# One fused kernel, its opening rearranged: reciprocal copies, expert ticks and the second block's attention change places

## The reference

```
xn = layernorm(x)
s  = causal softmax attention(xn), 16 heads of 64, projected back to 128
f  = shared expert(xn) + routed expert(xn)   # top 1 of 8, gate = sigmoid(score), width 352
x  = x + s * silu(f)
xn = layernorm(x)
s  = linear attention(xn), 16 heads of 8, causal cumulative sums
f  = two layers of local attention (8 heads of 64, window 64) and gated MLP, on xn
x  = x + s * silu(f)
```

## Time and profile before

| what | us |
|---|---|
| three runs, median (lowest to highest) | 2015.17 (2014.45 to 2017.05) |
| the profiled execution | 2009.89 |
| its span, first to last instruction | 2008.1 |
| TensorE busy | 1741.9 |
| VectorE, ScalarE busy | 1256.6, 1191.0 |
| GpSimd busy | 851.9 |

### The profile page before, as it was taken

How to read it: one execution, slowest core, us unless ns; L and a number is a source line. 1 busy time by engine, 2 the same in 40 slices (tenths; PEclk the granted TensorE clock), 3 DMA queues, 4 the chain that set the end, 5 groups by cost and what they waited for, 6 DMA issues and landing times.

```text
span 2008.1 us, 38006 instructions
## 1 busy us (share of the span) xinstructions
PE 1741.9 (87%) x12538; PEld 1123.2 (56%) x12538; DVE 1256.6 (63%) x4105; ACT 1191.0 (59%) x3559; POOL 851.9 (42%) x985
## 2 busy tenths in 40 slices
PE   6699989998989888998999898988899798785776
PEld 5378754654566546664566456654566455463454
DVE  5244547566675567666766667666766665857764
ACT  3554547566756675657666575666665665453643
POOL 3622226533535343532554353533353255534640
PEclk9999999999989999999999999999999897897978
DMA  8256500000000000000000000000000000000000
GB/s 245 71 180 211 176 16 4 9 1 1 7 1 17 1 7 1 17 1 1 7 1 17 1 7 1 17 1 6 1 7 6 1 7 1 1 7 1 1 1 11
DMA packets 50012, 53.78 MB, mean 27 GB/s; under 512 B 6546, under 2 KB 42396, under 8 KB 49820
## 3 DMA queue, kind: packets, MB, share of 16 engines
q0 software_dynamic: 7808, 27.79, 4.3%
q1 hardware_dynamic: 42012, 23.56, 4.1%
HBM read 41.90 MB, written 9.44 MB: 26 GB/s over the span
## 4 chain that ended last, share of the span: by engine, by line
PE 46%; DVE 20%; ACT 8%; issue 7%; POOL 1%; DVEq 0%; ACTq 0%; POOLq 0%
PE ps L610 5%; PE ps L672 5%; PE ps L756 3%; DVE p L1081 3%; PE ps L589 3%; PE ps L569 3%; DVE big L1264 3%; PE ps L630 3%; PE ps L579 3%; DVE ss L1260 2%; PE ps L807 2%; PE ps L798 2%; PE ps L644 2%; PE ps L654 2%; PE ps L800 2%
## 5 line engine op out<-in xcount | busy, mean ns | idle before, releaser
L1378 POOL COPY rdx<-rden 128x256 f32<-128x256 f32 x256 | 99.6, 418 | 624.4 <-DVE rden L1098 620.0
L1081 DVE CUSTOM_DVE_ANT_0 p<-ps,mask 128x128 f32<-128x128 f32 (+1 forms) x512 | 152.2, 353 | 197.9 <-PE ps L602 176.0
L1081 DVE CUSTOM_DVE_ANT_0 p<-ps,mask,rr 128x128 f32<-128x128 f32 x512 | 148.8, 347 | 168.9 <-PE ps L598 168.8
L610 PE MATMUL ps<-ident,p 128*128 128x128 f32 x1280 | 219.4, 293 | 37.4 <-ACT p L899 30.0
L899 ACT ACTIVATE p<-p,nmax 128x128 f32<-128x128 f32 (+1 forms) x512 | 226.3, 442 | 0.0
L756 PE MATMUL ps<-wqkv,hT 128*128 128x512 f32 x384 | 196.4, 618 | 31.1 <-ACT big L978 25.9
L913 ACT ACTIVATE pt<-ps 128x384 f32<-128x384 f32 (+1 forms) x256 | 111.6, 436 | 180.7 <-PE ps L610 171.5
L898 ACT ACTIVATE p<-p,nmax 128x128 f32<-128x128 f32 x512 | 200.2, 391 | 22.1 <-DVE nmax L1081 21.4
L610 PEld LDWEIGHTS ps<-ident,p 128*128 128x128 f32 x1280 | 140.7, 145 | 116.8 <-issue 101.6
L579 PE MATMUL ps<-ident,big 128*128 128x128 f32 x512 | 86.2, 308 | 80.1 <-DVE big L1269 35.5
L1092 DVE COPY pt<-ps 128x384 f32<-128x384 f32 (+1 forms) x256 | 124.5, 486 | 49.0 <-PE ps L610 45.9
(11 more groups left out here) (260 smaller groups left out, 4060.7 us busy)
## 6 DMA issues: line engine op xcount, KB each, us to landing
slots_in<-xn SPq DMA_DIRECT2D x1, 2560.0 KB, 12.9
v<-slots_in SPq DMA_DIRECT2D x20, 128.0 KB
slots_out<-v SPq DMA_DIRECT2D x20, 128.0 KB
big<-in_x SPq DMA_DIRECT2D x4, 512.0 KB, 5.8
x<-in_x SPq DMA_DIRECT2D x8, 256.0 KB, 3.7
out_x<-x SPq DMA_DIRECT2D x8, 256.0 KB, 2.3
wqkv<-in_wqkv SPq DMA_DIRECT2D x2, 768.0 KB
xn<-in_x SPq DMA_DIRECT2D x6, 256.0 KB, 3.2
```

The lines of the kernel that those rows point to most:

```text
L610: last = nc.tensor.transpose(bank[:, j * P:(j + 1) * P], c.p[:, u % 4, j * P:(j + 1) * P], c.ident[:, :])
L1081: last = V.tensor_tensor_reduce(out=c.p[:, u % 4, a:b], in0=bank[:, a:b], in1=mask, scale=scale, scalar=3e38, op0=ALU.add, op1=ALU.min, ac ...
```

## The change

Four edits. The body of GpSimd's `expand` becomes a function `spread` that any engine can run; VectorE runs it for pairs 0 to 4, right behind `inverse`, and GpSimd for the others. The experts start at `e_at` 10 instead of 8, all their segments two ticks later. The list of ticks is laid out anew: steps 0 to 15 in ticks 0 to 15, then 16 to 29 empty, steps 16 to 33 in ticks 30 to 47, 48 empty, step 34 in tick 49. The plan is two ticks longer, and from step 34 on its list is the one of before, two ticks later. `totals` on TensorE (the first of two products that rank the tokens) is issued one value product earlier. Segments that follow: experts in ticks 10 to 31, `tables` stays in tick 9 and now stands ahead of the first `wg`; `ffn` of block 0 in 32 to 34, `down0` in 35, `ln1` in 37, `ln1n` in 38, `xT` in 39, `qkv` of block 0 in 41 to 44.

```diff
+EXPERTS_AT = 10
+EARLY_PAIRS = EXPERTS_AT // 2
@@ lay_out
-        e_at = 8
+        e_at = EXPERTS_AT
         start = e_at + SLOT_PAIRS + 6
-        self.fill(start - 2, range(16, 22))
-        self.ticks += [None] * 7
-        self.fill(8, ())
+        self.fill(start - 2, range(16, 30))
+        self.fill(15, ())
@@ tensor
     for t in range(TILES):
-        if t == 3:
+        if t == 2:
             totals()
         values_of_tokens(0, 0, t)
@@ vector
+    def expand(pair):
+        dve.wait_ge(c.rden_ready, pair + 1)
+        if pair:
+            dve.wait_ge(c.mm_full, mm.full("m", pair - 1))
+        spread(V, c).then_inc(c.rdx_ready, 1)
@@
                 inverse(plan.step(tick - 1))
+                if plan.step(tick - 1).pair < EARLY_PAIRS:
+                    expand(plan.step(tick - 1).pair)
@@
+def spread(eng, c):
+    rd = c.rden[:, :].rearrange("p (s h i) -> p s i h", s=2, h=2)
+    for sq in range(2):
+        out = c.rdx[:, sq * SEQ:(sq + 1) * SEQ].rearrange("p (i h d) -> p i h d", i=2, h=2)
+        last = eng.tensor_copy(out, rd[:, sq, :, :].unsqueeze(3).to_broadcast([P, 2, 2, HD]))
+    return last
@@ gpsimd
-        rd = c.rden[:, :].rearrange("p (s h i) -> p s i h", s=2, h=2)
-        for sq in range(2):
-            out = c.rdx[:, sq * SEQ:(sq + 1) * SEQ].rearrange("p (i h d) -> p i h d", i=2, h=2)
-            last = G.tensor_copy(out, rd[:, sq, :, :].unsqueeze(3).to_broadcast([P, 2, 2, HD]))
-        last.then_inc(c.rdx_ready, 1)
+        spread(G, c).then_inc(c.rdx_ready, 1)
@@
-        if (st := plan.step(tick - 1)) and st.s == 1:
+        if (st := plan.step(tick - 1)) and st.s == 1 and st.pair >= EARLY_PAIRS:
             expand(st.pair)
```

## The result

The changed kernel is slower: 2033.45 us median (2030.08 to 2034.47, 4 runs) against 2014.81 us (2011.03 to 2017.05, 4 runs) beside it. The ratio is 1.0091, 95% interval 1.0078 to 1.0104. I had forecast 2007.1 within 1998.5 to 2017.0, and gave "slower" 0.16. The profiled execution took 2030.08 us, its span 2028.3 (before: 2009.89 and 2008.1).

The account below looks back on a forecast made before the run. TensorE, busy 87% of the span, was taken as the bound. Up to step 34 the terms summed to -10.8 + 7.2 - 6.0 + 1.5 = -8.1 us, taking the 2015.17 us median to 2007.1, range 1998.5 to 2017.

Parts of the forecast that it names:

- The stop for the tokens: At tick 8, TensorE's 10.91 us wait for the first expert pair's sorted tokens would go: -10.9 us.
- half clock: Behind the token stop, about 4.8 us of TensorE work at half speed would return to full speed: -2.4 us.
- late weights: First expert pair's weight gathers, now queued behind `tables` on GpSimd, would arrive late for tick 11: +1.0 us, 0 to 4.
- Late hand-offs: Between 57 and 95 us, ScalarE and VectorE take up TensorE results late; booked +1.5 us, from -6 to far above.
- rival B: Slower: unbroken scattering multiplies late hand-offs in ticks 2 to 8; 2027 us, or 2016 if milder; chance 0.13.
- My own sign of being wrong: The forecast would be wrong if the "remote" waits added more than 5 us.
- Experts alone: Ticks 16 to 29 without attention: seven more ticks idling fully, 1.03 us of idle in such a tick: +7.2 us.
- The layer-norm part: Empty ticks 32 to 38 filled by attention; whitening wait falls from 7.25 to about 3 us: -6.0 us.
- tick 48: The new empty tick before step 34 would cost 0, filled by ffn matmuls and the value product.
- rival C: Token stop only renamed: weights 4 to 6 us late at tick 11, lower clock behind; 2012 to 2014 us; chance 0.12.
- Rival E: Slower: expert ticks alone paced by DMA, deciding above 6.2 us a tick; 2020 us at 6.5; chance 0.10.
- The copies: Ten early copies on VectorE: path cost 0, 1.5 us if uncovered; blocking with scatters at most 0.96 us a time.

Follow-up runs that it names:

- e10b: Kernel before, with GpSimd waiting ahead of each tick's scatters until VectorE has taken up the previous step's logits (the wait didn't bind): ratio 1.0027 to the kernel before.
- e1: Kernel before, with the reciprocal copies of pairs 0 to 3 moved to VectorE and `totals` one value earlier: ratio 1.0027 to the kernel before.
- e2: Changed kernel with all reciprocal copies back on GpSimd, new order kept: ratio 1.0056 to the kernel before.
- e13b: Kernel before's order, copies on GpSimd, with experts from tick 10 and nothing else moved relative to them: ratio 0.9945 to the kernel before.
- e4: Changed kernel with the 32 indirect scatters replaced by plain stores of the same rows from SyncE, tokens unsorted: ratio 0.9967 to the kernel before.
- e5: Kernel before with the 32 indirect scatters replaced by plain stores of the same rows from SyncE, tokens unsorted: ratio 0.9851 to the kernel before.
- e6: Changed kernel with each scatter cut to 16 rows: ratio 1.0053 to the kernel before.
- e7: Changed kernel with each scatter writing 128 rows of 64 bytes to a buffer of its own: ratio 1.0058 to the kernel before.

## Why the prediction was wrong

**The stop for the tokens (-10.9, half clock -2.4): right where nothing else intervened.** Without holds the scatters ended at 87.3, the very time I had worked out, no stop was left, and TensorE's clock stayed at full speed. The gain at the first expert product is 5.2 + 7.1 = 12.3 us, where these two terms less the 2.5 of the attention-only ticks and the late weights are 10.8. But I had its cause wrong. I put 9.7 us of the scatters' time down to GpSimd's own queue. Without holds the scatters with copies between them take 42.2 us (e10b), without copies 40.4; in the kernel before they took 50.0. So 1.9 us were the copies. The other 7.8 were holds: GpSimd waited for a reciprocal because VectorE had itself been held up, by 7.99 us until 70.27 in the kernel before.

**Late hand-offs (+1.5): the step that failed first.** In the recorded pair SyncE could issue the first token load only at 96.94, not at 89 (the last scatter started at 94.70), and the first expert product came 11.2 us later with 7.1 us of steps more behind it: 4.1 lost, where the sum had 9.3 gained. That is 13.4 us. Its kind and place are those of rival B, and so is its half clock (granted 0.50 between 70 and 75 us, with no product in it). I gave B 0.13. My own sign of being wrong came up: the "remote" waits of 40 to 110 us add up to 44 us where the kernel before has 35, and the longest grew from 9.5 to 19.5. I had seen that holds ended near pauses, but held against it that one ended in the midst and many hand-offs were prompt, and booked the term at nearly nothing for want of a cause. A term with no known cause should have had the widest bounds of the sum, and most weight on growth, since the change lengthened the only activity that coincided with it. B is only half of it: the unbroken run by itself costs 0.27% (e1), and the new order with the old copies brings holds of its own and costs 0.56% (e2), which I had not seen.

**Experts alone (+7.2): right.** Idle 2.45 became 10.30, +7.9; the single wait is 1.03 us, as in rows 10.

**The layer-norm part (-6.0, and tick 48 at 0): wrong by itself.** The wait for the whitening came out at 3.65, I had about 3. But a new stop of 4.68 us at 354.52 took its place: TensorE had the shared expert's products next and waited for VectorE to take up the logits of the step before, while VectorE was busy with layer work for some 6 us. In all idle time fell by 2.1. Busy time should have fallen by two steps (7.1) less the 3.7 us that tick 48 puts ahead of step 34, and fell by 0.1, which makes +3.3. The half clock came back in it: 5.2 us against 3.4 when added up as for e13b, so at most 1.7 of the 3.3; the rest has no row. So the term was about +1.2, not -6.0, and tick 48 about +3.7 at step 34, not 0. The part of the mistake that was judgement: I counted what the filled ticks cover and did not ask what the attention placed there takes from VectorE, which the layer chain and the masks share.

**Late weights (+1.0, rival C): small.** Without holds TensorE waited 0.88 and 0.29 us for the weights. In the recorded pair the stops at the first expert products are 1.51 us, put down to "issue", and 1.15, for ScalarE's copy. Rival E did not occur: 5.50 us a tick. Attention-only ticks +1.5: nothing in the runs without holds speaks against it.

**The copies: 0 on the path without holds.** A pair took VectorE 0.68 us at 55.27 and 0.49 at 80.83, both beside scatters, and 0.49 each time in e4, where there are none. So the block of up to 0.96 us each that I had bounded from the rule on the shared port (the Trainium skill, Advanced Engine Details and Errata, Mode Summary) did not come: at most 0.2 for a pair, and the scatters kept their 1.26 us. The row for that bound I had also read wrongly: VectorE was not still beside the minimum of 0.86 us but ran `masked` (300.86 to 302.1). Where there are holds e1, the copies alone, costs 0.27%. In its trace 20 scatters go in a row where the kernel before has 8.

The sum at step 34 without holds, with the terms of the recorded pair behind the experts: -12.3 + 7.9 + 1.2 + 3.7 = +0.5; measured +0.6 (345.8 in the changed kernel against 345.1 in e10b). With holds +4.1 stands in place of -12.3, which makes 16.9; measured 16.8, but there every term is read from the same pair, so it tests nothing. Step 34 at 345.8 is also the 346 that I forecast, and that is luck: I took the 8 us from a kernel that had holds, and without them the kernel before has it at 345.1 to 347.4 (four profiles).

The 3.7 us should come back behind step 34. Without holds they don't show: SyncE stores block 0 at 616.0 to 620.8 in the profiles of the old order (four) and of the new one (three). In the recorded pair the distance is 14.0 us there (641.63 against 627.64). Behind it a block takes anything from 216 to 224 us in these profiles, though the plan is the same. So the 20.2 us at the pair's end can't be told from 14.0, and what lies between the 14.0 and the 18.6 of the medians stays open.

So where no holds occur the right forecast was "within 0.2%" (1.0008), and where they do "slower".

## What to carry to other kernels

Before an unexplained delay is booked at its old size, ask which activity it coincides with and whether the change makes more of that. Filling idle ticks with other work is worth only what the shared engines have left: read the neighbouring chain's own engine before counting the cover. And look at the kernel before in more than one group of runs: the cheapest sign here was its own median, 2015 in one group and 2004 in another, and the same changed kernel came out at 1.0091 in the first kind and 1.0008 in the second.

## What the runs showed of the hardware

While GpSimd issued indirect transfers one behind the other (1.26 us each), results of TensorE reached ScalarE and VectorE late in three of six groups, by 17 us in the changed kernel. All waits above 6.1 us ended 0 to 4.3 us behind the end of such a run; shorter ones ended inside runs too. In the changed kernel the result that came 17 us late was finished when nine transfers had been issued. It did not depend on rows (16 or 128) or bytes (64 or 512 a row). It grew with the number in a row, scatters or gathers: no "remote" wait beside two gathers, 2.2 us inside four (e5), 5.4 behind six (e6), 18.6 behind twenty scatters (e1, e7). It did not occur in the scatters' stretch when SyncE moved the same data (e4, e5). In the other three groups runs of over 30 in a row, in four profiles, did nothing of the kind. What distinguishes the groups is open: neither the program nor its order does, and the chip number alone does not. An indirect transfer's cost on GpSimd hardly depends on its rows: 0.85 us for 16, 0.96 for 128.
